# Softmax maxima of both heads of a pair in one pass, and q and k projected two units ahead

## What is computed

```python
def mha(xq, ctx, wq, wk, wv, wo, bo):          # H = 16 heads of DH = 64
    q = (xq @ wq).reshape(b, sq, H, DH).transpose(0, 2, 1, 3)
    k = (ctx @ wk).reshape(b, sk, H, DH).transpose(0, 2, 1, 3)
    v = (ctx @ wv).reshape(b, sk, H, DH).transpose(0, 2, 1, 3)
    attn = softmax(einsum('bhqd,bhkd->bhqk', q, k) / sqrt(DH))
    out = einsum('bhqk,bhkd->bhqd', attn, v).transpose(0, 2, 1, 3).reshape(b, sq, H * DH)
    return out @ wo + bo

h1 = adaln(x, t, norm1_w, norm1_b); x = mha(h1, h1, ...) + x        # self attention, 1024 keys
h2 = adaln(x, t, norm2_w, norm2_b); x = mha(h2, context, ...) + x   # cross attention, 77 keys
h3 = adaln(x, t, norm3_w, norm3_b); x = glu_ff(h3, ...) + x
# then x + bitlinear FFN of layernorm(x)
```

## Time and profile before

| | us |
|---|---|
| median of 3 executions | 1493.94 (1485.58 to 1496.99) |
| the profiled execution: its span, first to last instruction (the profile gives no other time of its own) | 1488.2 |
| self attention, batch 0 (8 units) | 102 to 476 |
| self attention, batch 1 (8 units) | 508 to 895 |
| cross attention, both batches with the output projection between | 923 to 1165 |
| mean granted TensorE clock, of full speed | 0.895 |

### The profile page before, as it was taken

The page is one execution under the profiler, slowest core; times in us unless marked ns, Lnnn a source line. Parts: engine busy times, 40 slices in busy tenths (PEclk is TensorE's granted clock), DMA queues, the critical chain, the costliest instruction groups (busy, mean ns, idle before and its releaser), DMA issues. The chain is left out here.

```text
span 1488.2 us, 35319 instructions
## 1 busy us (share of the span) xinstructions
PE 1217.3 (82%) x12739; PEld 762.7 (51%) x12739; DVE 975.8 (66%) x1908; ACT 609.8 (41%) x898; POOL 580.0 (39%) x558
## 2 busy tenths in 40 slices
PE   2579989899998899898999877788788589995555
PEld 0226546566556566555655546455555455553333
DVE  6466657767676676576666846876777566435885
ACT  2324444444443244444444531443143223334665
POOL 5215545565554456454655523211311150004441
PEclk9569999999999899999999988998898689996666
DMA  6301120211101021111112021234023400000000
GB/s 231 93 6 44 44 44 2 45 45 44 44 20 26 1 45 44 45 21 25 44 44 44 13 62 31 59 64 118 9 63 67 156 1 0 0 0 1 18 18 22
DMA packets 41847, 63.46 MB, mean 43 GB/s; under 512 B 11459, under 2 KB 22383, under 8 KB 41461
## 3 DMA queue, kind: packets, MB, share of 16 engines
q1 hardware_dynamic: 39088, 59.16, 15.9%
q10 hardware_dynamic: 2629, 2.41, 0.6%
HBM read 20.63 MB, written 2.10 MB: 15 GB/s over the span
## 5 line engine op out<-in xcount | busy, mean ns | idle before, releaser
L1118 POOL TENSOR_TENSOR exps_rest<-exps 128x1024 f16<-128x1024 f32 (+1 forms) x235 | 433.2, 1843 | 541.6 <-ACT exps L931 537.6
L931 ACT ACTIVATE exps<-scores 128x1024 f32<-128x1024 f32 (+1 forms) x320 | 299.8, 938 | 249.9 <-PE scores L653 244.9
L1301 DVE TENSOR_REDUCE maxes<-mixed 128x1 f32<-128x512 f32 x512 | 335.4, 684 | 61.9 <-PE mixed L625 60.1
L673 PE MATMUL outs<-values,exps 128*128 128x65 f16 (+1 forms) x2176 | 230.9, 194 | 17.6 <-DVE exps_rest L1325 11.0
L652 PE MATMUL scores<-head_operands 128*128 128x512 f16 (+1 forms) x576 | 227.6, 395 | 20.9 <-issue 13.1
L674 PE MATMUL outs<-values,exps 128*128 128x64 f16 (+1 forms) x2176 | 231.0, 193 | 0.0
L675 PE MATMUL outs<-values,exps_rest 128*128 128x65 f16 (+1 forms) x2176 | 230.6, 195 | 0.0
L653 PE MATMUL scores<-head_operands 128*128 128x512 f16 (+1 forms) x576 | 227.0, 394 | 0.0
L673 PEld LDWEIGHTS outs<-values,exps 128*128 128x128 bf16 (+1 forms) x2176 | 202.8, 99 | 44.4 <-DVE exps_rest L1325 18.2
L674 PEld LDWEIGHTS outs<-values,exps 128*128 128x128 bf16 (+1 forms) x2176 | 202.2, 98 | 24.0 <-issue 0.3
L625 PE MATMUL mixed<-head_operands 128*128 128x512 f16 x512 | 185.5, 394 | 21.2 <-DMA head_operands<-qk_pairs 12.5
(11 more groups left out here) (165 smaller groups left out, 1767.2 us busy)
## 6 DMA issues: line engine op xcount, KB each, us to landing
head_operands<-qk_pairs SPq DMA_DIRECT2D x128, 256.0 KB, 4.5
head_operands<-qk_pairs SPq DMA_DIRECT2D x32, 128.0 KB, 2.6
stage<-in_L_xcond_ff_w_dram SPq DMA_DIRECT2D x3, 1024.0 KB, 5.7
residual<-in_x_dram SPq DMA_DIRECT2D x4, 512.0 KB, 10.2
stage<-in_L_ffn_w_dram SPq DMA_DIRECT2D x2, 1024.0 KB, 6.5
head_operands<-in_x_dram SPq DMA_DIRECT2D x1, 2048.0 KB, 8.3
out_dram<-out_tile SPq DMA_DIRECT2D x16, 128.0 KB, 1.7
exps<-in_L_xcond_norm_w_dram ACTq DMA_DIRECT2D x3, 512.0 KB
```

What stands on the lines that cost most here:

```text
L673: mm(o, eb[:, sl], vb[:, DH:VW], start=(kt == 0 and q == 0), stop=False, skip_group_check=True)
L931: A(E[0:a.ks, c % RING, 0:n], SP_[c % 2][0:a.ks, 0:n], ACT.Exp, scale=SCALE).then_inc(s.exps, 1)
L1118: G.tensor_tensor(R[0:a.ks, c % RING, 0:n], e, e.bitcast(BF16).rearrange("p (n two) -> p n two", two=2)[:, :, 1], ALU.subtract).then_inc(s ...
L1301: V.tensor_reduce(mx[:, h, t, kh:kh + 1], m[:, :], AX_X, ALU.max).then_inc(s.maxed, 1)
```

## The change

- One pass for maxima now covers both heads of the pair. Each head has a matmul of its own over 64 rows, with the high parts alone (`MAIN[h]`: rows 0 to 63 for head 0, rows 64 to 127 for head 1), and writes its own one of two neighbouring banks; one reduction on VectorE reads both banks. Self attention has 16 passes per unit in place of 32, cross attention 2 in place of 4. The two banks are one buffer for every pass (`with_banks` gives bank 0).
- For head 1 the layout of `HB` is turned over: its own rows are 64 to 127, and low parts, zeros and the extra row stand in rows 0 to 63.
- One row transpose (16 columns in place of 8) and one copy per unit, and then two DMAs.
- Self attention projects q and k two units ahead, in slots 8 to 11. Its restack waits as cross attention's does. Passes stand in slots 1 to 12, the row in slot 13.
- The prologue has the passes of unit 0 and the q and k projections of units 0 and 1.

```diff
-            for i, n in enumerate((2, 1, 2, 1, 2)):
-                put(i, 0, *m[1][k:k + n])
+            for i, n in enumerate((1, 1, 1, 2, 1, 1, 2, 1, 1, 2, 1, 2)):
+                put(i + 1, 1, *m[k:k + n])
                 k += n
-            put(5, 0, ("row", 1))
+            put(13, 1, ("row",))
+            put(2, 1, ("v", 0))
+            put(5, 1, ("v", 1))
             for i, x in enumerate([("q", 0), ("q", 1), ("k", 0), ("k", 1)]):
-                put(i, 1, x)
...
+                put(8 + i, 2, x)
...
-        self.ahead = 1 if self.kt > 1 else 2
+        self.ahead = 2
...
             if x[0] in ("max", "row"):
-                out.append((du, x, turn % 2))
-                turn += 1
+                out.append((du, x, 0))
...
                         if (t, kh) == (0, 0):
-                            pe.wait_ge(s.heads[h], 16 * a.restack_dmas * (v.g + 1) + CREDIT)
+                            for h in range(2):
+                                pe.wait_ge(s.heads[h], 16 * a.restack_dmas * (v.g + 1) + CREDIT)
                         if a.kt > 1:
-                            last = mm(m[:, :], hb[:, QS, t * P:(t + 1) * P], hb[:, KH, kh * HALF:(kh + 1) * HALF],
-                                      start=True, stop=True)
+                            for h in range(2):
+                                hb = HB[MAIN[h], v.par, h, :, :]
+                                last = mm(M_[h], hb[:, QS, t * P:(t + 1) * P], hb[:, KH, kh * HALF:(kh + 1) * HALF],
+                                          start=True, stop=True)
...
+                        heads = m.rearrange("p (h n) -> p h n", h=2)
                         if a.kt > 1:
-                            V.tensor_reduce(mx[:, h, t, kh:kh + 1], m[:, :], AX_X, ALU.max).then_inc(s.maxed, 1)
+                            V.tensor_reduce(mx[:, :, t, kh], heads, AX_X, ALU.max).then_inc(s.maxed, 1)
```

More of the change, by code:

```diff
@@ L100, in __init__ @@
             self.k_parts, self.v_tiles, self.max_parts = 1, 1, 1
-            m = [[("max", h, t, 0) for t in range(2)] for h in range(2)]
+            m = [("max", t, 0) for t in range(2)]
             put(0, 2, ("q", 0), ("q", 1))
-            put(1, 1, m[0][0])
+            put(1, 1, m[0])
             put(1, 2, ("k", 0))
-            put(1, 1, m[0][1], m[1][0])
-            put(2, 1, ("row", 0), m[1][1], ("v", 0), ("row", 1))
+            put(1, 1, m[1])
+            put(2, 1, ("v", 0), ("row",))
             put(4, 0, ("out", 0), ("out", 1))
@@ L111, in __init__ @@
         self.restacked = ("k", self.k_parts - 1)
-        self.ahead = 1 if self.kt > 1 else 2
+        self.ahead = 2
         self.restack_dmas = 3 if self.kt > 1 else 4
         self.v_items = self.kt // self.v_tiles
-        self.max_items = len(m[0])
+        self.max_items = len(m)
         order = [x for slot in self.slots for x in slot]
-        pro = [(d, x) for d in range(self.ahead - 1) for du, x in order if du == 2]
-        pro += [(self.ahead - 1, x) for du, x in order if du == 2]
-        pro += [(0, x) for du, x in order if du == 1]
+        pro = [(0, x) for du, x in order if du == 2]
+        behind = [(1, x) for du, x in order if du == 2]
+        for k, x in enumerate([(0, x) for du, x in order if du == 1]):
+            if self.kt == 1 or (k > 5 and k % 2 == 0 and behind):
+                pro += behind if self.kt == 1 else behind[:1]
+                behind = [] if self.kt == 1 else behind[1:]
+            pro.append(x)
         self.prologue = self.with_banks(pro)
@@ L151, in max_no @@
     def max_no(self, what):
-        _, h, t, kh = what
-        return h * self.max_items + (t * 2 + kh if self.kt > 1 else t)
+        _, t, kh = what
+        return t * 2 + kh if self.kt > 1 else t
     def item_no(self, u, left, k):
@@ L294, in build @@
         PV_ = [ps(f"outs{i}", [P, 512]) for i in range(2)]
-        M_ = [ps(f"mixed{i}", [P, 512]) for i in range(2)]
-        ITEM = [M_[0], M_[1], PV_[1], SP_[1][:, HALF:2 * HALF]]
+        MM = ps("mixed", [P, 1024])
+        M_ = [MM[:, i * 512:(i + 1) * 512] for i in range(2)]
+        ITEM = [MM[:, :], None, PV_[1], SP_[1][:, HALF:2 * HALF]]
+        MAIN = [slice(0, DH), slice(DH, P)]
+        OTHER = [slice(DH, P), slice(0, DH)]
+        EXTRA = [slice(DH, DH + 1), slice(0, 1)]
         def outs(a, c):
@@ L699, in prologue @@
                         item(u, u.ahead(du), what, bank, a.before(k, a.prologue))
-                    for bank in range(2 + a.outer_banks):
+                    for bank in (0, *range(2, 2 + a.outer_banks)):
                         du, what = [x[:2] for x in a.prologue if x[2] == bank][-1]
@@ L899, in item @@
                     if kind in ("q", "k"):
-                        n = v.g if a.ahead == 1 else v.g - 1
+                        n = v.g if a.kt > 1 else v.g - 1
                         for h in range(2):
```

80 lines of the change are left out of this document (37 added, 43 removed).

## The result

The kernel with the change takes 1569.2 us (median of 4 runs, 1566.1 to 1577.6) against 1492.1 for the kernel before, a ratio of 1.053 with a 95% interval of 1.050 to 1.057. Forecast were 1543 us, in a range of 1497 to 1595: slower, as forecast, but by 77 us in place of 49.

What follows compares the result with a forecast made beforehand. TensorE's in-order queue was taken as the bound. On the span, 14 + 25 + 19 - 4.6 - 4 - 8 + 8 = +49 made 1488.2 into 1537; 5.7 for the runs' median gave 1543 us, range 1497 to 1595.

Steps and rivals of the forecast that it cites:

- The overlap of the two matmuls: In each pass for maxima, both matmuls run at once: 16 passes of 0.22 us replace 32 of 0.215.
- the round trip: Self attention, one pair of banks for every pass: passes can start 1.70 us apart at best.
- The rival without an overlap: A pass's two matmuls run one behind the other, a pass costs 0.43 us: 1599 us in all, chance 0.11.
- the faster one: Waits are covered, with passes under about 1.6 us apart and the restack under 7.6: 1441 us, chance 0.13.
- Near no change: Single buffer costs as forecast, but the restack comes in time (-25) and the prologue is shorter (-12): 1506 us, chance 0.12.
- The step on changing the array's division: Self attention: 0.04 us at each end of seven passes, 0.6 a unit, 8 us in all; 12 with 0.06.
- the second rival: Each change of shape empties the array: tail of 0.165 us at both ends of seven passes, 1570 us, chance 0.16.
- The step on the passes: Self attention: with overlapping matmuls, TensorE's own work falls by 3.4 us a unit, to 37.9 with one row transpose less.
- The restack's wait: Self attention, slot 1: data after 10.4 us where TensorE has 7.6, so 2.8 us in nine units, 25 us.
- The jumps: Self attention: four units behind a loop's jump back hide the restack's wait, as TensorE stands about 2.9 us there anyway.
- Prologue: From first pass to first scores, 35 to 45 us in place of 21.1: 14 to 24 more, taken as 19.
- Cross attention: Two passes of 616 columns replace four of 308, with one row wait fewer: 8 us less, bounds 0 and 14.

Runs made afterwards that it cites:

- first run: The changed kernel, with the restack sending the parts a pass reads first and both heads' low parts last, on semaphores of their own: 1543.1 us, ratio 1.033.

## Why the prediction was right and where it was not

**Right.** The bound (TensorE's queue in order, with latency taking the place of work), the direction, the range. The overlap of the two matmuls and the price of a reduction (1.22), the round trip (1.75 for 1.70), its place (slot 10), the restack from its issue to the first pass: 10.68 us from the last scores' start, forecast 10.4.

```profile
267.93 5.71 SPq L488 DMA_DIRECT2D head_operands<-qk_pairs  x6
...
DMA  2000098989997996999988999999699895200000
```

Issued at 267.9, the data moves until about 276.7 (40 slices from 267.9 to 277.9), by the trace the last landing is signalled at 277.3, and the pass above starts at 277.39. (Read in the same two ways, end at 315.8 and 317.0; the prediction took 316.3 for the last packet.) The rival without an overlap is refuted by the trace, and the faster one by its own condition: 1.75 and 9.3 stand against its 1.6 and 7.6. Near no change is out too: the restack came too late nine times.

**The step on changing the array's division** is the one that failed most. It took 0.04 us at each end of seven passes, with 0.06 as the upper bound, from a transpose into 8 columns. Measured: 0.10 at each end. That row has another number of columns, and the pass has another number of rows, so it bounded nothing here. And the exit costs its 0.10 behind all 16 passes, waited for or not: 2.9 us a unit in place of 0.6. The Trainium skill (TensorEngine Tiling (Array Packing), Key Properties) has the rule that a new tiling mode drains the array. The trace agrees that it costs something at each end. It doesn't show the whole tail of 0.165 that the second rival made of the rule. The prediction's own sign for that rival, a value matmul more than 0.3 behind the start of its pass, did appear (0.32), but a full tail would have been 0.38. So per end the truth lies between my term and the rival's; per unit, 2.9 is above the rival's 2.3, since it too counted seven passes. That its 1570 was met is luck, as waits, prologue and jumps were off as well.

**The step on the passes** ("TensorE's own work falls by 3.4 us") follows: it fell by 3.4 and rose by 2.9. In exchange the waits for reductions were fewer, 4.9 us for 6.8, since work that takes longer on the queue covers more of a round trip. In the view, which counts from modelled ends, the waits for `maxes` are 3.6 us a unit, below the 6 to 7 named as a sign.

**The restack's wait** was sized rightly (nine of 2.1 to 3.3 us by the trace, nine of 2.8 forecast), but costed at its own length. What was left out is TensorE's clock behind it: 1.2 GHz for 3.4 us, 1.5 us of time more. Eight of the nine waits have it behind them.

**The jumps.** The forecast hid the restack in the pause of "about 2.9 us" and counted it at nothing there. The four pauses grew from 13.1 to 18.8 us with the restack in them. The slow clock behind them is no new cost: 13.5 us of work at 1.2 GHz behind the four jumps, and 14.0 before. The four units behind a jump take 54.3 us on average, where the forecast makes it 51.2 (before 49.7, and 1.5 for buffer and shape): 12 us. Of these 5.7 are the pauses, and nearly 4 what the table above has for shape, shorter waits and the end of a unit; the rest isn't traced to anything. The nine that wait for the restack missed by 2.3 on average, 20 us. Together that is 32 of the 38 by which self attention missed.

**Prologue** +13.6 for +19: from first pass to first scores it takes 42.6 us, inside the 35 to 45, but its first pass starts 7.9 us earlier (73.1 against 81.0), which wasn't seen. **Cross attention** -12.7 for -8, inside its bounds of 0 to 14.

**What the 77 us are**, by the experiments: the restack's wait with its clock 26 (first run), the pairs with their shape and single buffer 54 (1543.1 against 1489.1), the early projection itself about 0, the last two net of the parts named above. How the 54 split between shape and buffer isn't shown, as the two hide each other: in the unit above it is 2.9 us of shape and 4.9 of waits, less the 3.4 of matmuls saved and the short waits of before. A pair with two buffers wasn't tried: it needs four banks where `mixed` has two.

## What to carry to other kernels

Two small matmuls that overlap save time only if the queue gets shorter: a lone pair in another shape among full ones pays at both of its ends, here nearly as much as it saved, so measure from the start of the last matmul before it to the start of the first behind it. Where an in-order queue is the bound, a second buffer is worth more than fewer instructions: 2.5 us of waits against 28.6 and 77.0. And a wait or a move is costed with what follows it, the slower clock behind a wait and the transfers that now fall into a pause.

## What the runs showed of the hardware

- A change between matmuls over 128 rows and over 64 costs TensorE's queue 0.10 us at each end; from one matmul over 64 rows to the next there is none.
- A loop's jump back has a price that depends on the DMA traffic beside it: TensorE's pause is 2.9 to 3.8 us without other transfers, 4.4 to 5.2 with a transfer of some 0.7 MB in it. In 16 pauses of four kernels TensorE started 1.5 to 1.7 us after the last packet of instructions had landed, and that packet began 0.4 to 1.0 us after the last matmul without other transfers, 1.6 to 2.5 with them. Writing the loop out was worth 17 us on the kernel before, 16 to 19 on after, 27 on the pairs with room between them, and 23 to 28 on single passes with q and k two ahead.
- Eight of nine waits of 2.1 to 3.3 us had 3.4 us at 1.2 GHz with them, beginning from 0.3 us before the wait's end to 1.4 us behind it. In the unit whose starts were added up that cost 1.5 us more than the wait's length.
